# An attention kernel whose TensorE loop is written out, with values rounded in one GpSimd operation and the first keys and maxima on their own transfers

## The chip, the cores and the metric

One Trainium2 chip; the kernel runs on one of its cores. Five engines of that core have a part: TensorE (PE in the rows, its weight loads PEld), VectorE (DVE), ScalarE (ACT), GpSimd (POOL) and SyncE (SP), which issues the transfers. The metric is the device time of one execution in microseconds, lower is better.

## The reference

1600 queries (16 x 100 rows of 256) attend to 23104 keys made from a context, in 16 heads of 16, with queries, keys, probabilities and values rounded to 8-bit grids; a feed-forward layer with 8 experts follows.

```python
kv = (cond @ Wkv + bkv).reshape(1, -1, 2, H, hd)        # H = 16 heads, hd = 16
q = _fq_sym(q * scale, axis=-1)                         # round(q / s) * s, s = max|q| / 127
k = _fq_sym(k, axis=-1)
v = _fq_sym(v, axis=2)                                  # one step for each head and column of v
attn = softmax(q @ k.T)                                 # 1600 x 23104 for each head
attn = _fq_unsigned(attn, axis=-1)                      # step = row maximum / 255
x = x + (attn @ v) @ Wp + bp
x = x + ffn(layernorm(x))                               # 8 experts, two for each row
```

## The kernel before

Each engine has one program written by hand; semaphores tie them together. There are four stages.

**Preparation** (0 to 486 us): 51 steps of 512 rows project queries, keys and values. Three bf16 parts of the keys go to memory as `kT_parts`, float values as `v_float`, whole-number queries as `q_int` (`sp.dma_start(qi_d...)`, line 768).

**Prologue** (486 to 723 us). Two chains run beside each other. In one, TensorE multiplies the queries of the first block with all keys of head 0, a job at a time: `job` (line 1431) writes a pair of psum banks, VectorE's `job` (1292) reduces them to maxima in `mpart`. There are 96 + 7 such jobs, and two pairs of banks. The keys come in three pieces (`load_k1`). In the other chain the values are rounded in nine chunks of 2560 KB: load `vin` (three buffers, `load_vin`), GpSimd multiplies by `vinv` in place (line 1058), VectorE adds and takes away `RNE` to round, writing `vo` in f16 (`round_values`, line 1320, at chunks `ROUND_AT` of the other chain), SyncE stores `vo` (two buffers, `store_vo`). After the last chunk GpSimd rounds off with small constants, a memset over `K3` (line 1083) and two over `y` and `xh` (1090, 1091), which wait for the last stores. Then the maxima of block 0 are transposed (`mT`) and loaded as three rows of `QT` by SyncE (`load_m`, 841, `load_m_tail`, 847).

**Main loop** (723 to 8122 us): 16 heads x 4 blocks of 400 queries. A block is three bodies (`body(h, b, c)`), each with 15 groups of four key tiles of 128. For each tile TensorE makes scores (line 1522; the 181st tile of a block, `KX`, at 1548 opens the block) in a ring of three psum banks, ScalarE takes their exponential (1186; 1170 for `KX`), GpSimd rounds four of them at a time (1105). TensorE sums the group before with `ones` (1489) and multiplies the one before that with the values (1499). Between the tiles stand 78 jobs (1434) that find the maxima for a later block. All engines run the same nest through `bodies`: a hardware loop over `h` (line 402), in it one over `b` (404), and in that three bodies written out. Wait values are computed in registers. A tile with `j` in `PAIRS` waits for the exponential that frees the bank of its successor too, and the successor has no wait.

**Feed-forward layer** (8122 to 8735 us).

## Time and profile before

| | us |
|---|---|
| median of 3 runs | 8744.33 |
| lowest, highest | 8737.29, 8747.74 |
| the profiled execution | 8736.84 |
| its span | 8735.0 |
| preparation, prologue, main loop, feed-forward layer | 486, 237, 7399, 613 |
| TensorE busy | 93% of the span |
| VectorE, ScalarE, GpSimd busy | 77%, 62%, 60% |

A row of a group gives count, busy time, mean duration of one and the idle time ahead of it with the instruction that ended it. The chain of waits is read from the last instruction backwards: each piece is what held up the next. "issue" there is time in which an engine had nothing to wait for that the profile shows. Rows of PEldq, ACTq, DVEq and POOLq are instructions that the engine's sequencer handles alone (branches, register operations, waits).

### The profile page before, as it was taken

The page shows a single profiled execution, that of the slowest core. Times are in us where ns is not written, and L with a number is a line of the kernel's source. Part 1 is how long each engine was busy: PE and PEld are TensorE (multiplying, and loading weights), DVE is VectorE, ACT ScalarE, POOL GpSimd, SP SyncE. Part 2 cuts the span into 40 slices and gives each one's busy share as a digit, 9 for nine tenths or more (in the row PEclk, how much of TensorE's full clock was granted, in tenths as well). Part 3 has the DMA queues.
Part 4 walks back from the last instruction along what each step waited for, and adds up shares of the span by engine and source line. Part 5 has one row for each costly group of instructions (what it writes and reads, how often), then busy time and mean ns, then how long its engine had stood idle before and what let it go on. Part 6 is the DMA issues. An engine that isn't in the chain of part 4 may idle for free.

```text
span 8735.0 us, 208420 instructions
## 1 busy us (share of the span) xinstructions
PE 8114.0 (93%) x60567; PEld 2495.4 (29%) x60567; DVE 6754.0 (77%) x6609; ACT 5422.6 (62%) x12187; POOL 5211.0 (60%) x3573
## 2 busy tenths in 40 slices
PE   8937999999999999999999999999999999999688
PEld 4512222222222222222222222222222222222343
DVE  8977777777777777777777777777777777777666
ACT  2304667666666666666666666666666666666333
POOL 5765556555655566555555566555555566555356
PEclk9958999999999999999999999999999999999799
DMA  5663020202020201111110202020202021110000
GB/s 163 209 201 76 24 36 23 38 19 42 17 44 15 44 17 39 22 35 26 31 30 25 36 23 38 22 38 19 43 14 46 15 41 21 38 21 25 11 4 4
DMA packets 324119, 357.12 MB, mean 41 GB/s; under 512 B 66266, under 2 KB 306246, under 8 KB 315174
## 3 DMA queue, kind: packets, MB, share of 16 engines
q1 hardware_dynamic: 323046, 343.01, 17.0%
q8 instruction: 649, 10.63, 0.5%
q14 instruction: 424, 3.47, 0.1%
HBM read 264.31 MB, written 78.41 MB: 39 GB/s over the span
## 4 chain that ended last, share of the span: by engine, by line
PE 87%; issue 5%; DVE 4%; POOL 2%; DMA 1%; ACT 1%; SPq 0%; DVEq 0%; POOLq 0%; ACTq 0%
PE psum L1522 30%; PE psum L1489 27%; PE psum L1434 17%; PE psum L1499 6%; PE psum L1404 3%; POOL mix L431 1%; DVE mpart L1293 1%; DVE act_c L572 1%; PE psum L693 1%; PE psum L1481 1%; DVE vo L1320 1%; PE psum L1567 1%; PE psum L1416 0%; PE psum L666 0%; PE psum L1392 0%
## 5 line engine op out<-in xcount | busy, mean ns | idle before, releaser
L1293 DVE TENSOR_REDUCE mpart<-psum 128x1 f32<-128x978 f32 (+1 forms) x5095 | 5774.9, 1171 | 1581.6 <-PE psum L1434 1510.9
L1186 ACT ACTIVATE y<-psum 128x400 f32<-128x400 f32 x11520 | 5006.4, 506 | 2013.8 <-PE psum L1522 1922.2
L1105 POOL TENSOR_SCALAR xh<-y 128x1600 f16<-128x1600 f32 x2880 | 4397.8, 1527 | 2751.1 <-PE psum L1499 1698.0
L1522 PE MATMUL psum<-QT,K 99*128 x11520 | 3046.6, 346 | 39.1 <-ACT y L1186 37.8
L1489 PE MATMUL psum<-y,ones 128*17 128x400 f32 x23048 | 2573.5, 513 | 0.0
L1434 PE MATMUL psum<-K,QS 48*128 48x489 bf16 x8464 | 1510.4, 389 | 156.8 <-DVE mpart L1293 92.9
L1522 PEld LDWEIGHTS psum<-QT,K 99*128 99x128 bf16 x11520 | 796.8, 98 | 2381.6 <-ACT y L1186 1771.6
L1499 PE MATMUL psum<-xh,vwin 128*16 128x400 f16 x11528 | 1027.9, 338 | 0.5 <-POOL xh L1105 0.5
L1434 PEld LDWEIGHTS psum<-K,QS 48*128 48x128 bf16 x8464 | 372.5, 94 | 1202.1 <-issue 952.1
L1489 PEld LDWEIGHTS psum<-y,ones 128*17 128x17 f32 x23048 | 403.8, 96 | 794.3 <-issue 794.0
L1499 PEld LDWEIGHTS psum<-xh,vwin 128*16 128x16 f16 x11528 | 324.5, 91 | 637.6 <-POOL xh L1105 322.1
L572 DVE TENSOR_TENSOR act_c<-act_a,combB 128x400 f32<-128x400 f32 x256 | 314.3, 1300 | 53.1 <-ACT act_a L465 53.1
L1404 PE MATMUL psum<-wkv,srcT 128*128 128x512 f32 x736 | 324.7, 594 | 0.0
L431 POOL TENSOR_TENSOR mix<-mix,act_c 128x400 f32<-128x400 f32 x224 | 294.8, 1352 | 2.3 <-DVE act_c L572 2.3
L465 ACT ACTIVATE act_a<-psum,b1c 128x400 f32<-128x400 f32 x256 | 152.2, 594 | 166.5 <-PE psum L682 102.4
L1548 PE MATMUL psum<-QT,KX 99*128 x64 | 30.8, 481 | 235.4 <-issue 235.4
L682 PE MATMUL psum<-t1d,b1T 128*128 128x400 f32 x512 | 216.5, 531 | 18.6 <-ACT act_a L465 16.8
L1170 ACT ACTIVATE yx<-psum 128x400 f32<-128x400 f32 x64 | 32.3, 504 | 280.5 <-PE psum L1548 280.5
L427 POOL TENSOR_SCALAR mix<-act_c 128x400 f32<-128x400 f32 x32 | 24.1, 764 | 266.8 <-DVE act_c L572 266.8
L1404 PEld LDWEIGHTS psum<-wkv,srcT 128*128 128x128 f32 x736 | 136.8, 191 | 154.8 <-issue 154.8
L1028 POOL TENSOR_TENSOR kq<-kv,kinv 128x256 f32<-128x256 f32 x200 | 118.1, 623 | 89.2 <-DVE kinv L1242 89.2
L1434 PE MATMUL psum<-K,QL 48*128 48x489 bf16 x910 | 163.4, 379 | 3.3 <-DVE mpart L1293 2.8
(189 smaller groups left out, 2562.4 us busy)
## 6 DMA issues: line engine op xcount, KB each, us to landing
K<-kT_parts SPq DMA_DIRECT2D x288, 240.0 KB, 8.3
vwin<-v_int SPq DMA_DIRECT2D x579, 80.0 KB, 1.9
K1X<-kT_parts SPq DMA_DIRECT2D x772, 45.8 KB
kT_parts<-part SPq DMA_DIRECT2D x135, 256.0 KB, 3.0
src<-in_ctx_dram SPq DMA_DIRECT2D x46, 512.0 KB, 4.4
v_float<-kv SPq DMA_DIRECT2D x45, 512.0 KB, 5.0
vin<-v_float SPq DMA_DIRECT2D x9, 2560.0 KB, 14.6
K<-kT_parts SPq DMA_DIRECT2D x34, 450.9 KB
```

Of the source, the lines that this page charges most:

```text
L431: pool.tensor_tensor(mix[:, f, :], mix[:, f, :], act_c[:, i % CR, :], ALU.add).then_inc(mixed, 1)
L465: act.activation(act_a[:, i % AR, :], psum[:, bank, 0:QB], ACT.Gelu_apprx_tanh, bias=b1c[:, f:f + 1])\
L572: dve.tensor_tensor(act_c[:, i % CR, :], act_a[:, i % AR, :], combB[:, e, :], ALU.mult)\
L682: pe.matmul(psum[:, bank, 0:QB], b1T[:, f * P:(f + 1) * P], t1d[:, e, :], start=False, stop=True, skip_group_check=True).then_inc(p_ready, 1)
L1105: pool.tensor_scalar(xh[:, g % YR, :, :], y[:, g % YR, :, :], INT_STEP, 0.0, ALU.mult, ALU.add)\
L1186: act.activation(y[:, s % YR, j, :], s2_bank(GT * s + j), ACT.Exp).then_inc(exp_done, 1)
L1293: dve.tensor_reduce(mpart[:, t, column], buf[:, :, 0:CHALF], AX.XY, ALU.max).then_inc(s1_free, 1)
L1404: last = pe.matmul(kv_psum(t)[:, 0:width], srcT[:, k.r, c, t * P:(t + 1) * P], w, start=(c == 0), stop=(c == DC - 1))
L1434: last = pe.matmul(buf[:, k, 0:CHALF], tile[top:end, :], keys[top:end, :], start=True, stop=True)
L1489: last = pe.matmul(ACC[32 * j:32 * j + HD + 1, :], ones[:], y[:, g % YR, j, :], start=(start and j > 0), stop=True, skip_group_check=True)
L1499: last = pe.matmul(ACC[32 * j:32 * j + HD, :], vwin[:, g % GROUPS // 5, GT * (g % 5) + j, :], xh[:, g % YR, j, :], start=False, stop=True, ...
L1522: pe.matmul(s2_bank(t), K3[0:MROW, c * REGION + t * P:c * REGION + (t + 1) * P], queries, start=True, stop=True).then_inc(s2_ready, 1)
```

## The change

TensorE's nest becomes Python loops: 64 blocks x 3 bodies stand in the program, with no branch between them and constants as wait values; the other four engines keep their hardware loops. `PAIRS` goes: every tile waits for its own bank. In the prologue GpSimd multiplies by `vinv * 2^-24` and writes f16 `vo` straight, which rounds to whole steps of 2^-24, and VectorE's nine roundings go; `ones` carries the other factor. The keys of the first two chunks are loaded alone and before the queries, the store of `q_int` is split in two halves with a semaphore each, and the second half is moved behind the first value load and the rest of the first key piece. The first maxima are loaded by ScalarE's queue.

```diff
-PAIRS = (0,)
+K1_FIRST = CSTEP + CHALF
-ROUND_AT = (5, 7, 9, 11, 13, 15, 17, 19, 21)
...
             sp.wait_ge(qi_copied, DC)
-            for i in range(3):
-                for c in range(DC):
-                    sp.dma_start(qi_d[H // DC * c:H // DC * (c + 1), i, :, :], qintT[:, c, :]).then_inc(qi_stored, 16)
+            def store_qi(c):
+                for i in range(3):
+                    sp.dma_start(qi_d[H // DC * c:H // DC * (c + 1), i, :, :], qintT[:, c, :]).then_inc(qi_stored[c], 16)
+
+            store_qi(0)
             wait_prep_stores(sp)
-            sp.wait_ge(qi_stored, 48 * DC)
...
+            load_keys(0, 0, K1_FIRST, k1_first)
+            sp.wait_ge(qi_stored[0], 48)
             load_qs(QS, 0, 0, qs_in)
-            load_k1(0, 0)
             load_qs(QX, 0, BLOCKS * MAIN, qx_in)
             load_vin(0)
+            load_keys(0, K1_FIRST, K1_EDGES[1], k1_in[0])
+            store_qi(1)
+            load_vin(1)
             load_k1(0, 1)
-            load_vin(1)
+            sp.wait_ge(qi_stored[1], 48)
             load_vin(2)
             load_k1(0, 2)
...
-            sp.wait_ge(mt_copied, 1)
-            load_m(0, 0)
-            load_m_tail(0)
...
-                pool.memset(w[:, HD:HD + 1], INT_STEP).then_inc(zeroed, 1)
+                pool.memset(w[:, HD:HD + 1], INT_STEP * INT_STEP).then_inc(zeroed, 1)
...
-            pool.wait_ge(v_scaled, 2)
+            pool.wait_ge(v_scaled, 3)
             for c in range(9):
                 pool.wait_ge(vin_in[c % 3], 16 * (c // 3 + 1))
-                pool.tensor_tensor(vin[:, c % 3, :, :], vin[:, c % 3, :, :],
-                                   vinv[:].unsqueeze(1).to_broadcast([P, VCH, D]), ALU.mult).then_inc(vin_scaled, 1)
+                if c >= 2:
+                    pool.wait_ge(vo_stored[c % 2], 16 * (c // 2))
+                pool.tensor_tensor(vo[:, c % 2, :, :, :].rearrange("p h t d -> p t h d"),
+                                   vin[:, c % 3, :, :].rearrange("p t (h d) -> p t h d", h=H),
+                                   vinv[:].rearrange("p (h d) -> p h d", h=H).unsqueeze(1).to_broadcast([P, VCH, H, HD]),
+                                   ALU.mult).then_inc(vo_ready, 1)
...
             mt_copy(0, 0, 0, 4 * CHUNKS, s1_buf(4 * CHUNKS))
+            act.wait_ge(qs_split, 2)
+            load_m(act, 0, 0)
+            load_m_tail(act, 0)
...
+            dve.wait_ge(v_scaled, 2)
+            dve.tensor_scalar(vinv[:], vinv[:], INT_STEP, None, ALU.mult).then_inc(v_scaled, 1)
...
-                if chunk in ROUND_AT:
-                    round_values(ROUND_AT.index(chunk))
...
-                if piece_of(chunk) >= 0:
+                if chunk == 0:
+                    pe.wait_ge(k1_first, 32)
+                elif chunk == 2:
+                    pe.wait_ge(k1_in[0], 32)
+                elif piece_of(chunk) >= 0:
                     pe.wait_ge(k1_in[piece_of(chunk)], 32)
...
-                        if j in PAIRS:
-                            pe.wait_ge(exp_done, T + t + 2)
-                        elif j - 1 not in PAIRS:
-                            pe.wait_ge(exp_done, T + t + 1)
+                        pe.wait_ge(exp_done, T + t + 1)
...
-            bodies(pe, body, head_start)
+            for h in range(H):
+                head_start(h)
+                for b in range(BLOCKS):
+                    for c in range(BODY_C):
+                        body(h, b, c)
```

TensorE, from the last value group of a block to the first of the next. Before, the end of the loop's text (the branches go back to the second piece):

```order
L1499 MATMUL psum<-xh,vwin 16x400 x3
L404 REGISTER_ALU
L404 COMPARE_AND_BRANCH
L402 REGISTER_ALU
L402 COMPARE_AND_BRANCH
```

Before, the start of the loop's text:

```order
L404 UNCONDITIONAL_BRANCH [waits kx_in]
L1511 ISA [waits k_in0]
L1547 ISA [waits m_in]
L1548 ISA [waits exp_done]
L1548 ISA
L1548 MATMUL psum<-QT,KX 128x400
L1522 MATMUL psum<-QT,K 128x400 [waits exp_done]
L1522 MATMUL psum<-QT,K 128x400
```

Now, the same place between blocks 0 and 1:

```order
L1502 MATMUL psum<-xh,vwin 16x400 x3
L1548 MATMUL psum<-QT,KX 128x400 [waits exp_done,m_in,k_in0]
L1522 MATMUL psum<-QT,K 128x400 [waits exp_done] x2
L1433 MATMUL psum<-K,QL 128x489 [waits s1_free]
```

The branches and register operations are gone, and each of the two tiles has a wait of its own.

GpSimd in the prologue, chunks 1 to 3 of the values. Before:

```order
L1058 TENSOR_TENSOR vin<-vin,vinv 128x5120 [waits vin_in1]
L1058 TENSOR_TENSOR vin<-vin,vinv 128x5120 [waits vin_in2]
L1058 TENSOR_TENSOR vin<-vin,vinv 128x5120 [waits vin_in0]
```

Now:

```order
L1064 TENSOR_TENSOR vo<-vin,vinv 128x20x16x16 [waits vin_in1]
L1064 TENSOR_TENSOR vo<-vin,vinv 128x20x16x16 [waits vo_stored0,vin_in2]
L1064 TENSOR_TENSOR vo<-vin,vinv 128x20x16x16 [waits vo_stored1,vin_in0]
```

From chunk 2 on GpSimd itself now waits for the store that empties the `vo` buffer; VectorE did so before.

SyncE at the start of the prologue. Before:

```order
L768 DMA q_int<-qintT 8x16x1664 x5
L797 DMA QS<-q_int 48x384 [waits v_stored2,qi_stored,k_stored2,qs_split,v_stored1,k_turned,k_stored1,v_max,v_stored0,k_stored0]
L797 DMA QS<-q_int 48x384
L810 DMA K<-kT_parts 48x1x4810 x2
L797 DMA QX<-q_int 48x128 x2
L826 DMA vin<-v_float 128x5x1024
L810 DMA K<-kT_parts 48x1x4329 x2
L826 DMA vin<-v_float 128x5x1024 x2
```

Now:

```order
L821 DMA K<-kT_parts 48x1x970 [waits v_stored2,k_stored2,qs_split,v_stored1,k_turned,k_stored1,v_max,v_stored0,k_stored0]
L821 DMA K<-kT_parts 48x1x970
L809 DMA QS<-q_int 48x384 [waits qi_stored0]
L809 DMA QS<-q_int 48x384
L809 DMA QX<-q_int 48x128 x2
L840 DMA vin<-v_float 128x5x1024
L821 DMA K<-kT_parts 48x1x3840 x2
L779 DMA q_int<-qintT 8x16x1664 x3
L840 DMA vin<-v_float 128x5x1024
```

The first keys and queries stand ahead of half of the `q_int` store, and the second value load stands behind the other half.

## Rows read from the trace of the kernel before

**Rows 1.** The page: busy time, the chain by engine, TensorE's instruction transfers.

```profile
PE 8114.0 (93%) x60567; PEld 2495.4 (29%) x60567; DVE 6754.0 (77%) x6609; ACT 5422.6 (62%) x12187; POOL 5211.0 (60%) x3573
...
PE 87%; issue 5%; DVE 4%; POOL 2%; DMA 1%; ACT 1%; SPq 0%; DVEq 0%; POOLq 0%; ACTq 0%
...
q8 instruction: 649, 10.63, 0.5%
```

**Rows 2.** Waits of 720 to 8120 us: total, times, longest.

```profile
PE psum L1548 <- issue: 235.4, 64, 18.9
```

**Rows 3.** Line 404, 4060 to 4080 us: ns (min/median/max), first and last start.

```profile
L404 PEldq COMPARE_BRANCH  x1: 3457/3457/3457, 4069.4 to 4069.4; - x1
...
L404 ACTq COMPARE_BRANCH  x1: 45/45/45, 4069.6 to 4069.6; - x1
...
L404 DVEq COMPARE_BRANCH  x1: 56/56/56, 4069.9 to 4069.9; - x1
L404 DVEq FUSED_REGOPS  x1: 160/160/160, 4070.2 to 4070.2; - x1
...
L404 ACTq FUSED_REGOPS  x1: 133/133/133, 4072.1 to 4072.1; - x1
```

**Rows 4.** Chain of waits, 4070 to 4100 us: start, length, what.

```profile
4070.73 3.06 issue
...
4074.96 0.93 PE psum L1434 x4
4075.89 0.78 PE psum L1522 x2
4076.68 1.47 PE psum L1489 x8
...
4078.48 0.78 PE psum L1522 x2
...
4090.02 0.56 PE psum L1434 x4
4090.58 0.45 PE psum L1522 x2
4091.02 0.80 PE psum L1489 x8
```

**Rows 5.** Stretches: length, busy time by engine, granted clock, DMA share, GB/s.

```profile
4074.00:4076.00 2.00, 2.00 (x8) 0.42 (x7) 0.47 (x1) 1.30 (x3) 0.53 (x1) 0.50 0.00 0
...
4080.00:4082.00 2.00, 1.98 (x14) 0.58 (x12) 2.00 (x3) 1.85 (x5) 0.69 (x1) 1.00 0.03 8
```

**Rows 6.** Timeline, 4060 to 4080 us: start, length, engine, instruction, idle before.

```profile
4074.33 0.50 ACT L1170 ACTIVATE yx<-psum 128x400 f32<-128x400 f32 x1 [4.10 <-PE psum L1548]
```

**Rows 7.** Groups, 486 to 723 us: busy, mean ns, idle before.

```profile
L1293 DVE TENSOR_REDUCE mpart<-psum 128x1 f32<-128x978 f32 x103 | 112.5, 1161 | 34.4 <-PE psum L1434 34.4
...
L1320 DVE TENSOR_SCALAR vo<-vin 128x5120 f16<-128x5120 f32 x9 | 56.2, 6246 | 2.2 <-POOL vin L1058 2.2
```

**Rows 8.** Line 1058: ns of one, min/median/max.

```profile
L1058 POOL TENSOR_TENSOR vin<-vin,vinv x9: 10952/13017/13555, 536.2 to 659.3; 128x5120 f32<-128x5120 f32 x9
```

**Rows 9.** Chain of waits of the whole span, in the prologue.

```profile
525.46 32.10 DMA vin<-v_float
...
681.56 2.73 DVE vo L1320
...
721.49 1.52 issue
```

**Rows 10.** Timeline of GpSimd, 530 to 725 us.

```profile
693.23 0.30 POOL L1063 MEMSET vox<- 64x256 f16 x1 [19.75 <-DVE vox L1332]
```

**Rows 11.** Stretches of the prologue.

```profile
600.00:640.00 40.00, 13.55 (x46) 2.38 (x46) 40.00 (x25) 0.00 (x0) 34.70 (x4) 0.50 0.90 300
```

**Rows 12.** The page: transfers, with KB of one and median us to landing.

```profile
vin<-v_float SPq DMA_DIRECT2D x9, 2560.0 KB, 14.6
...
v_int<-vo SPq DMA_DIRECT2D x9, 1280.0 KB, 13.9
```

More of the change, by code:

```diff
@@ L315, in build @@
         v_absmax, v_scaled = sem("v_absmax"), sem("v_scaled")
-        vin_scaled, vo_ready = sem("vin_scaled"), sem("vo_ready")
+        vo_ready = sem("vo_ready")
         vin_in, vo_stored = [sem(f"vin_in{j}") for j in range(3)], [sem(f"vo_stored{j}") for j in range(2)]
-        vx_in, vx_scaled, vx_round, vx_zero, vx_stored = sem("vx_in"), sem("vx_scaled"), sem("vx_round"), sem("vx_zero"), sem("vx_stored")
-        qi_kept, qs_kept, qi_turned, qi_copied, qi_stored = (
-            sem("qi_kept"), sem("qs_kept"), sem("qi_turned"), sem("qi_copied"), sem("qi_stored"))
+        vx_in, vx_round, vx_zero, vx_stored = sem("vx_in"), sem("vx_round"), sem("vx_zero"), sem("vx_stored")
+        qi_kept, qs_kept, qi_turned, qi_copied = sem("qi_kept"), sem("qs_kept"), sem("qi_turned"), sem("qi_copied")
+        qi_stored = [sem(f"qi_stored{c}") for c in range(DC)]
+        k1_first = sem("k1_first")
         k1_in, k1x_in = [sem(f"k1_in{r}") for r in range(3)], [sem(f"k1x_in{j}") for j in range(2)]
@@ L373, in key_window, with load_m, load_m_tail @@
             return keys[:, CSTEP * chunk:CSTEP * chunk + CHALF]
+        def load_m(eng, ring, b):
+            for r in range(3):
+                eng.dma_start(QT[NROW + r:NROW + r + 1, ring, ds(b * QB, MAIN)].rearrange("r (t c) -> r t c", c=P),
+                             mT[(PT + 1) * r:(PT + 1) * r + PT, :]).then_inc(m_in, 16)
+        def load_m_tail(eng, ring):
+            for r in range(3):
+                row = (PT + 1) * r + PT
+                eng.dma_start(QT[NROW + r:NROW + r + 1, ring, :].rearrange("r (b k) -> r b k", b=BLOCKS)[:, :, MAIN:QB],
+                             mT[row:row + 1, 0:BLOCKS * TAIL].rearrange("r (b k) -> r b k", b=BLOCKS)).then_inc(mx_in, 16)
         def s2_bank(j):
@@ L805, in load_tiles, with load_keys, load_k1 @@
                     load_qs(dst, (h + (turn + ahead) // BLOCKS) % H, (turn + ahead) % BLOCKS * MAIN, arrived)
-            def load_k1(head, piece):
-                first, end = K1_EDGES[piece], K1_EDGES[piece + 1]
+            def load_keys(head, first, end, arrived):
                 for k, (top, bottom) in enumerate(HALVES):
                     sp.dma_start(K1[top:bottom, first:end], kT_d[:, ds(head * HD, HD), HALF * k + first:HALF * k + end])\
-                        .then_inc(k1_in[piece], 16)
+                        .then_inc(arrived, 16)
+            def load_k1(head, piece):
+                load_keys(head, K1_EDGES[piece], K1_EDGES[piece + 1], k1_in[piece])
             def load_k1x(head, chunk, j):
@@ L837, in load_values @@
                              v_d[ds(body, 1), :, :].rearrange("a p n -> (a p) n")).then_inc(v_in[q], 16)
-            def load_m(ring, b):
-                for r in range(3):
-                    sp.dma_start(QT[NROW + r:NROW + r + 1, ring, ds(b * QB, MAIN)].rearrange("r (t c) -> r t c", c=P),
-                                 mT[(PT + 1) * r:(PT + 1) * r + PT, :]).then_inc(m_in, 16)
-            def load_m_tail(ring):
-                for r in range(3):
-                    row = (PT + 1) * r + PT
-                    sp.dma_start(QT[NROW + r:NROW + r + 1, ring, :].rearrange("r (b k) -> r b k", b=BLOCKS)[:, :, MAIN:QB],
-                                 mT[row:row + 1, 0:BLOCKS * TAIL].rearrange("r (b k) -> r b k", b=BLOCKS)).then_inc(mx_in, 16)
+            load_keys(0, 0, K1_FIRST, k1_first)
+            sp.wait_ge(qi_stored[0], 48)
             load_qs(QS, 0, 0, qs_in)
-            load_k1(0, 0)
             load_qs(QX, 0, BLOCKS * MAIN, qx_in)
             load_vin(0)
+            load_keys(0, K1_FIRST, K1_EDGES[1], k1_in[0])
+            store_qi(1)
+            load_vin(1)
             load_k1(0, 1)
-            load_vin(1)
+            sp.wait_ge(qi_stored[1], 48)
             load_vin(2)
@@ L938, in block @@
                             sp.sem_inc(sp_passed, 1)
-                            load_m((h + (1 if end else 0)) % 3, 0 if end else b + 1)
+                            load_m(sp, (h + (1 if end else 0)) % 3, 0 if end else b + 1)
                             if end:
-                                load_m_tail((h + 1) % 3)
+                                load_m_tail(sp, (h + 1) % 3)
                         if q == 2 and c == BODY_C - 1:
```

12 lines of the change are left out of this document (1 added, 11 removed).

## The prediction

> **What bounds the kernel now.** I read the page first: TensorE is busy for 93% of the span and makes 87% of the chain, with "issue" at 5% next [rows 1]. So TensorE's own work is the bound, and the 5% are time in which it waited for no data. The list of waits says where most of that is: the tile that opens a block (line 1548) finds TensorE idle for 235.4 us in 64 blocks [rows 2]. Without the first (18.9 us, the end of the prologue) that is 216.5 us over 63 block edges, 3.44 us each.
>
> The rows of line 404 at one edge say why [rows 3]. TensorE's branch back takes 3457 ns; VectorE's takes 56 ns and the next instruction stands there 0.3 us after it. ScalarE's branch takes 45 ns too, but its next instruction comes at 4072.1, 2.6 us after the branch at 4069.6. The long loops (TensorE, ScalarE) get their code anew at the branch, the short one doesn't. ScalarE's wait is covered today, because TensorE is away longer: it starts `KX` at 4073.79 [rows 4], and ScalarE is then idle on TensorE, not the other way round [rows 6].
>
> The second cost of an edge is the clock. It is granted at 0.50 behind the gap (the lower level, 1.2 GHz) and is back at 1.00 by 4080 [rows 5]. In the chain the same operations take 0.93, 0.78 and 1.47 us behind the gap and 0.56, 0.45 and 0.80 us later in the block [rows 4], a ratio of 1.81/3.18 = 0.57. The slow stretch runs from 4073.79 to 4078.48 + 0.78 = 4079.26, 5.47 us, and would take 3.1 us at full clock: 2.4 us lost. An edge costs 3.44 + 2.4 = 5.8 us.
>
> The prologue ends at 721.49 + 1.52 = 723.0 [rows 9]. Its chain goes through value load 1 (there at 525.46 + 32.10 = 557.6), then VectorE, which alternates 103 jobs (112.5 us) with nine roundings (56.2 us) [rows 7] and ends the last rounding at 681.56 + 2.73 = 684.3. GpSimd sits idle for 19.75 us on VectorE before its constants [rows 10], and from there to the first block it is 723.0 - 693.2 = 29.8 us of GpSimd's own work.
>
> **The loop written out.** The branch goes, 64 times: 63 gaps of 3.44 us, and the overlap of two matmuls that an idle engine lacks, 0.07 us (a pair of tiles takes 0.45 us where it follows other work). What is late next is ScalarE. It keeps its loop, and I expect its code at the same place after the branch. At this edge TensorE ends at 4070.73. It can do `KX`, two tiles and two jobs without ScalarE, 0.17 + 0.45 + 0.56 - 0.1 for the overlap, until about 4071.8; the next tile needs the bank that `KX` holds. ScalarE is ready at 4072.1 + 0.13 for the register operation and 0.1 for its wait, 4072.4, and needs 0.50 us for `KX` [rows 3, 6], so the bank is free at 4072.9. TensorE idles 1.1 us, and about 0.25 us more for the tile behind it, since ScalarE hands out banks one by one. That is 1.35 us here; for edges where the code comes later I take 1.5 on the mean (bounds 1.0 and 2.2: code half a microsecond sooner, or as late as the branch that TensorE itself pays, shorter by the lead that ScalarE has). VectorE, free at 4070.2, covers its two banks, and GpSimd isn't asked for before the next group.
>
> Does the clock still fall? The gap is cut from 3.06 us to 1.1, with work close before and behind it. Behind gaps of 3.06 it fell. The gaps inside a block (0.3 us and less) never let it fall. 1.1 us lies between, nearer to the second; I take no fall. The Trainium skill ("TensorE: Matmul & The Clock Gate", section "Why this matters for your kernels") asks for no idle gaps over about 3 us between bursts, or the clock goes to half; the trace agrees for 3.06 us, and no row shows 1.1 us.
>
> So an edge gives 3.44 + 2.4 + 0.07 - 1.5 = 4.4 us, and 63 of them 278 us (bounds 3.7 and 4.9: 233 and 309).
>
> The size of a loop that runs without new code can be read in the Trainium skill too ("Runtime: NRT & Kernel Launch", "Instruction fetch mechanics"): two blocks of 256 instructions for all engines but TensorE. ScalarE's loop has fewer than 512 instructions, and by that rule it would not fetch, the 1.5 us would fall away, and the kernel would take about 95 us less than my sum. The rows show a ScalarE that fetches, so the measurement decides.
>
> The constants cost and save nothing: register operations run on TensorE's sequencer, which reached the branch at 4069.4 while its array worked until 4070.73, so it is 1.3 us ahead. Waits of their own for the tiles of a pair: 0. The first tile of a pair waited for a bank that was free long before, and pairs with a wait on each take 0.45 us as those with one. Loads of keys, queries and maxima are in place before an edge today, and edges that come 3 us sooner relative to them leave that so for all but the second part of the maxima, which has about 1 us to spare at a head's start.
>
> **The prologue.** (a) VectorE loses 56.2 us of roundings and gets one multiplication of some 0.3 us before the prologue. Its chain is then 103 jobs of 1.09 us, 112 us. The first eight start early, the others wait for the rest of the first key piece; even if that came at 535 us, 95 jobs end at 640, before GpSimd's chain, so this side is free. (b) GpSimd takes one operation per chunk as before. Alone it takes 10.95 us, beside VectorE's rounding 13.55 [rows 8]; now it is alone. That its output is f16 in another order is not in the trace; I take 11 us (bounds 11 and 13.5). (c) The transfers: a chunk is 2560 KB in and 1280 KB out [rows 12], 3.84 MB. At the best rate of the prologue, 300 GB/s with a DMA share of 0.90 [rows 11], that is 12.8 us, more than GpSimd's 11. GpSimd's new wait for the store two chunks back asks for 13.9 + 11 us per two chunks [rows 12, 8], 12.5 each, with nothing queued behind it but its own next chunk, so it takes the same place. Chunks 1 to 5 go at 12.8 us, the last three, with no load beside them, at 11, and the key region that is loaded between takes 1.44 MB / 300 = 5 us: 64 + 33 + 5 = 102. (d) The start: queries and keys are issued about 8 us sooner, but value load 1 has gone behind the rest of the keys and half of `q_int`. It lands between 545 (all gained) and 557.6 (as now); I take 551. Last chunk at 551 + 102 = 653, 31 us sooner than 684.3. Behind it GpSimd has the small remainder (1 us) and its 29.8 us: first block at 684, instead of 723. The maxima on ScalarE's queue free SyncE for some 5 us that no one waits for. Gain 39 us; bounds 59 (545, all chunks at 11) and 21 (557.6, all at 13.5).
>
> **Sum.** 8735.0 - 278 - 39 = 8418 us of span, 8420 for an execution that is profiled (1.8 around the span). The median of before is 7.5 us above its profiled execution; half of that added gives 8424. With both bounds of the terms: 8370 to 8485.
>
> **Rivals.** (1) *The clock falls all the same.* ScalarE's gap of 1.1 to 1.6 us, near the smaller gaps around it, is enough. Then 63 x 2.4 = 151 us come back: 8575. For it: the slow stretch is long against the gap, so little may set it off. (2) *Another wait takes the whole place of the branch*, so an edge stays as it is and the prologue alone gains: 8705. It needs an engine that is ready only 3 us after TensorE's end; ScalarE at 1.4 us speaks against it. (3) *ScalarE's code comes sooner* once TensorE fetches none beside it, up to the rule above: 8329. (4) *Slower: the straight code stalls.* TensorE gets its code in 649 transfers of 16.4 KB [rows 1]; about 530 of them fall in the main loop, 8 a block. They were asked for inside a body before too, and no row there shows a stall. If each now held TensorE up, the limit is 317/530 = 0.6 us apiece; at the 3.4 us of a branch [rows 3] it would be 1800 us and 10200 in all. It would have to be something that a program written out has and a body written out hasn't.
>
> **How the numbers follow.** My forecast has 0.74, rival 1 has 0.12, rival 2 has 0.05, rival 3 has 0.05, rival 4 has 0.04. The range has to reach rival 1 to leave out no more than 2 in 10: 8370 to 8580, with 0.14 outside. A measurement of this kernel can tell 0.2% (17 us) from no change. Faster: 0.95; within 0.2%: 0.01; slower: 0.04.
>
> **What would show it.** In the changed kernel: no branch of TensorE in the main loop; `KX` without idle time before it; the third tile of a block waiting for ScalarE 1 to 1.6 us; ScalarE's first instruction of a block as late as now against its branch; granted clock 1.00 from the second group of the first block to the end of the loop. 111 us from block to block instead of 115.6. In the prologue: operations of 11 us on GpSimd, VectorE done by 640, the first block at 684. If the clock row shows a dip at each edge, rival 1 holds; if `KX` waits for "issue", rival 4; if value chunks run at 13 us or more, the f16 output or the store's wait was priced too low.

## The result and the profile of the changed kernel

The changed kernel takes 8446.6 us (median of 4 runs, 8446.4 to 8454.8) where the kernel before takes 8746.0 beside it (8737.3 to 8753.1): a ratio of 0.966, 95% interval 0.964 to 0.968, 299 us less. Forecast were 8424, with a range from 8370 to 8580. The profiled execution has a span of 8444.7 us, 290.3 less than the 8735.0 of before.

| Part, from the profiled executions | before | after | difference |
|---|---|---|---|
| first `KX` starts | 723.0 | 708.2 | -14.8 |
| 63 periods, from first to last `KX` | 7282.9 (115.60 each) | 7003.6 (111.17 each) | -279.3 |
| from the last `KX` to the end | 729.1 | 732.8 | +3.7 |

So the loop gave what was forecast (278) and the prologue 15 us of 39.

The page, against [rows 1]: TensorE works for less time and a larger share, ScalarE's part of the chain has gone from 1% to 2%, and TensorE's instruction transfers have fallen from 649 to 462.

```profile
span 8444.7 us, 192076 instructions
...
PE 7981.2 (95%) x60567; PEld 2495.3 (30%) x60567; DVE 6720.7 (80%) x6600; ACT 5409.1 (64%) x12187; POOL 5195.9 (62%) x3573
...
q8 instruction: 462, 7.57, 0.4%
...
PE 87%; issue 4%; DVE 2%; POOL 2%; ACT 2%; DMA 1%; SPq 1%; ACTq 0%; DVEq 0%; POOLq 0%
```

Waits from 690 to 8120 us (total, times, longest), the place of [rows 2]. The 235.4 us behind the branch are gone. Of the 85.2 us for line 1548, 53.4 are the one wait at the prologue's end; the rest is half a microsecond of weight load per block beside other work. New is the wait for `yx`: 69.1 us in 64 blocks, 1.08 each.

```profile
PEld psum L1548 <- issue: 85.2, 64, 53.4
...
PE psum L1522 <- ACT yx L1181: 69.1, 64, 1.6
```

One edge in the rows of the loop's line (now 415; ns, then first and last start), 4040 to 4050 us. TensorE has no row there. ScalarE's branch takes 45 ns and the register operation behind it stands 2.4 us later, as in [rows 3].

```profile
L415 ACTq COMPARE_BRANCH  x1: 45/45/45, 4043.7 to 4043.7; - x1
...
L415 ACTq FUSED_REGOPS  x1: 133/133/133, 4046.1 to 4046.1; - x1
```

The chain at that edge (start, length, what) goes through just that time, 1.73 us in which ScalarE waited for nothing that is shown, and on to `yx`:

```profile
4044.40 1.73 issue
4046.12 0.13 ACTq L415
...
4046.38 0.05 ACT yx L1181
```

Stretches of the edge (columns as in [rows 5]). TensorE works for 1.03 of the two microseconds from 4046 and its clock stays at 1.00; in [rows 5] it was at 0.50 behind the gap.

```profile
4044.00:4046.00 2.00, 2.00 (x19) 0.49 (x11) 1.60 (x3) 0.40 (x2) 1.34 (x1) 1.00 0.15 28
4046.00:4048.00 2.00, 1.03 (x12) 0.37 (x14) 2.00 (x2) 1.62 (x5) 0.72 (x2) 1.00 0.05 17
```

In the prologue, GpSimd's timeline (start, length, engine, what, idle before and its releaser): chunk 1 is in at 542.3, but chunk 2 waits 28 us, for a store.

```profile
542.34 10.97 POOL L1064 TENSOR_TENSOR vo<-vin,vinv 128x5120 f16<-128x5120 f32 x1 [19.02 <-DMA vin<-v_float]
581.56 10.96 POOL L1064 TENSOR_TENSOR vo<-vin,vinv 128x5120 f16<-128x5120 f32 x1 [28.25 <-DMA v_int<-vo]
...
625.16 21.88 POOL L1064 TENSOR_TENSOR vo<-vin,vinv 128x5120 f16<-128x5120 f32 x2 [7.47 <-DMA v_int<-vo]
657.30 21.88 POOL L1064 TENSOR_TENSOR vo<-vin,vinv 128x5120 f16<-128x5120 f32 x2 [10.27 <-DMA v_int<-vo]
```

SyncE's queue shows why. Chunk 0 was ready in `vo` at 523.3. SyncE then still had keys, queries and two more value loads to issue, and came to its store at 562.6; the data were out at 581.4.

```profile
534.98 12.14 SPq L821 DMA_DIRECT2D K<-kT_parts  x2
547.16 4.12 SPq L809 DMA_DIRECT2D QL<-q_int  x2
551.32 0.73 SPq L866 DMA_DIRECT2D vinx<-v_float_last  x1
552.10 9.99 SPq L830 DMA_DIRECT2D K1X<-kT_parts  x4
562.13 0.46 SPq L840 DMA_DIRECT2D vin<-v_float  x1
562.64 3.96 SPq L846 DMA_DIRECT2D v_int<-vo  x1
```

### The profile page after: what moved, and what is told of

The parts are those of the page before. It is cut to its first block, busy times and chain, and to the rows that moved or that the text cites. A ratio compares the mean times of both kernels' runs of the same rounds, so it can differ in the third digit from the quotient of the medians.

```text
span 8444.7 us, 192076 instructions
## 1 busy us (share of the span) xinstructions
PE 7981.2 (95%) x60567; PEld 2495.3 (30%) x60567; DVE 6720.7 (80%) x6600; ACT 5409.1 (64%) x12187; POOL 5195.9 (62%) x3573
## 4 chain that ended last, share of the span: by engine, by line
PE 87%; issue 4%; DVE 2%; POOL 2%; ACT 2%; DMA 1%; SPq 1%; ACTq 0%; DVEq 0%; POOLq 0%
PE psum L1522 30%; PE psum L1492 26%; PE psum L1433 17%; PE psum L1502 6%; PE psum L1403 3%; ACT y L1197 2%; POOL mix L442 1%; DVE act_c L583 1%; PE psum L704 1%; DMA v_int<-vo 1%; PE psum L1484 1%; PE psum L1567 1%; PE psum L1415 1%; PE psum L677 1%; PE psum L1391 0%
## 5 line engine op out<-in xcount | busy, mean ns | idle before, releaser
L1522 PE MATMUL psum<-QT,K 99*128 99x400 bf16 x11520 | 2991.8, 339 | 111.4 <-ACT yx L1181 69.1
L1492 PE MATMUL psum<-y,ones 128*17 128x400 f32 x23048 | 2528.5, 506 | 0.0
L1433 PE MATMUL psum<-K,QS 48*128 48x489 bf16 x8464 | 1481.9, 380 | 88.6 <-DVE mpart L1306 34.4
L1522 PEld LDWEIGHTS psum<-QT,K 99*128 99x128 bf16 x11520 | 798.7, 97 | 2413.4 <-ACT y L1197 1700.2
L1144 ACT ACTIVATE part<-rest 128x1024 bf16<-128x1024 f32 x50 | 52.9, 1058 | 168.0 <-DVE rest L1264 168.0
L1064 POOL TENSOR_TENSOR vo<-vin,vinv 128x5120 f16<-128x5120 f32 x9 | 98.6, 10963 | 84.4 <-DMA v_int<-vo 49.2
```

Source lines behind the costliest of these rows:

```text
L1433: last = pe.matmul(buf[:, k, 0:CHALF], tile[top:end, :], keys[top:end, :], start=True, stop=True)
L1492: last = pe.matmul(ACC[32 * j:32 * j + HD + 1, :], ones[:], y[:, g % YR, j, :], start=(start and j > 0), stop=True, skip_group_check=True)
L1522: pe.matmul(s2_bank(t), K3[0:MROW, c * REGION + t * P:c * REGION + (t + 1) * P], queries, start=True, stop=True).then_inc(s2_ready, 1)
```

## Experiments

Times are medians; the ratio is against the kernel before on the same chip, with its 95% interval. "Period" is the mean time from one `KX` to the next in the profiled execution, "first" the start of the first.

| Run | Time, us | Ratio | Span | First | Period |
|---|---|---|---|---|---|
| changed kernel | 8446.6 | 0.966 (0.964 to 0.968) | 8444.7 | 708.2 | 111.17 |
| e1_loop_alone | 8464.6 | 0.969 (0.967 to 0.970) | 8466.9 | 722.8 | 111.29 |
| e2_prologue_alone | 8761.7 | 1.003 (1.002 to 1.004) | 8767.4 | 706.6 | 116.33 |
| e6_prologue_pairs | 8734.2 | 0.999 (0.998 to 1.000) | 8730.1 | 707.8 | 115.65 |
| e4_gap_after_kx | 8674.9 | 0.994 (0.992 to 0.995) | 8663.1 | 706.7 | 114.62 |
| e8_gap_tile3 | 8561.1 | 0.980 (0.979 to 0.982) | 8544.9 | 707.8 | 112.75 |
| e3_act_out | 8450.6 | 0.967 (0.966 to 0.969) | 8450.2 | 707.8 | 111.27 |
| e5_act_out_sem | 8337.7 | 0.954 (0.953 to 0.956) | 8340.1 | 708.3 | 109.57 |
| e7_stores_on_act | 8445.7 | 0.967 (0.965 to 0.968) | 8446.6 | 700.7 | 111.37 |
| e9_constants_early | 8337.8 | 0.954 (0.953 to 0.956) | 8336.1 | 689.0 | 109.77 |
| e10_act_stores_consts | 8334.6 | 0.954 (0.953 to 0.955) | 8330.8 | 685.3 | 109.77 |
| e11_loads_behind | 8331.9 | 0.954 (0.952 to 0.955) | 8330.7 | 683.0 | 109.78 |
| e12_ffn_loads_late | 8317.5 | 0.951 (0.950 to 0.953) | 8318.9 | 684.0 | 109.59 |

### The two halves of the change apart

The loop alone, on the kernel before:

```diff
-            bodies(pe, body, head_start)
+            for h in range(H):
+                head_start(h)
+                for b in range(BLOCKS):
+                    for c in range(BODY_C):
+                        body(h, b, c)
```

> The kernel before with one edit: TensorE's loop nest written out (its pair waits, the prologue and all else stay). Theory (the two parts of the change add up, and the loop gives 4.4 us at each of 63 edges): 279 us less than before, 8735 - 279 = 8456 for the profiled span, 111.2 us from block to block, first block at 723. Rival (the first keys, the values and the constant waits of the tiles have a share in the gain of the loop): less than 270 us.

The period falls by 4.31 us, 272 us in 63, with the pair waits and the old prologue in place. That is the gain of the loop but for 8 us, of which 6 are in the clock (27 us at the lower clock at three edges, against 14 us at four). So the waits of their own for the two tiles of a pair are worth at most the 0.12 us per block that remain between the two, as forecast: nothing that can be told. The span is 268 us under that of before, 11 short of the theory's 279 and just inside the rival's "less than 270"; but only these 8 us are in the loop, and the clock explains 6 of them, so the reason that the rival gives is not shown.

The other half alone, the changed kernel with TensorE on its hardware loop:

```diff
-            for h in range(H):
-                head_start(h)
...
+            bodies(pe, body, head_start)
```

> The changed kernel with TensorE back on the hardware loop. Theory: the prologue's part alone, 723.0 - 708.2 = 15 us less than before (8720 of span), edges as before: 3.4 us idle, then the lower clock, 115.6 us from block to block. By the prediction's own term it would have been 39 us (8696). Rival (the time won in the prologue is lost again behind it, since later transfers meet others): no difference from before.

Neither held. The first block starts 16.4 us sooner, and the kernel is slower than before, by 0.3%. The period has grown to 116.33. The rows of TensorE's branch, 730 to 8000 us, of the kernel before and then of this one (ns, minimum/median/maximum):

```profile
L404 PEldq COMPARE_BRANCH  x62: 83/3614/4137, 833.5 to 7886.1; - x62
```

```profile
L415 PEldq COMPARE_BRANCH  x62: 82/4608/5157, 817.7 to 7914.1; - x62
```

A branch of 4.6 us instead of 3.6. What differs on TensorE in the loop is only that each tile of a pair has its wait, with a register operation each: 2873 instructions more in the trace than before, 45 a block. To see that it is this, I gave that kernel its pair waits back:

```diff
-                        pe.wait_ge(exp_done, T + t + 1)
+                        if j in PAIRS:
+                            pe.wait_ge(exp_done, T + t + 2)
+                        elif j - 1 not in PAIRS:
+                            pe.wait_ge(exp_done, T + t + 1)
```

> The kernel before with the prologue of the changed one, hardware loops and pair waits kept. It differs from e2_prologue_alone by the waits of the tiles alone. Theory (the wait per tile makes TensorE's loop 45 instructions a block longer, and its branch 4.6 us instead of 3.6): idle time at an edge back at 3.4 us, 115.6 us from block to block, first block at 707, 8718, 16 us less than before and 44 less than e2_prologue_alone. Rival (the prologue or its placement of loads slows the edges): 8762 as e2_prologue_alone.

```profile
L416 PEldq COMPARE_BRANCH  x63: 82/3637/4132, 818.4 to 7988.9; - x63
```

The theory held: 3.6 us again, the idle time at an edge back from 4.42 to 3.48, the period from 116.33 to 115.65, 27 us off the median. TensorE's instruction transfers fit it: 649 before, 702 in e2_prologue_alone, 649 again here. So the same waits are free in code written out and cost some 0.7 us a block in the loop, through what the branch back then takes. That it is the length of the code which sets this, and not where its pieces come to lie, is argued: one length was tried. Against the kernel before, the prologue is worth 0.1%, 8 us, with an interval that ends at nothing: the first block starts 15 us sooner, but from the last `KX` to the end it took 736.6 us here, for 729.1 before. This stretch took between 729.0 and 736.6 us in the profiles of this document, so a few microseconds of it can't be put down to an edit.

### How long may TensorE stand still

Rival 1 was that the clock falls at the shorter gaps too. Two versions of the changed kernel widen the gap with no branch in it, by a wait for GpSimd's operation on `yx`. The first, behind `KX`:

```diff
                         pe.matmul(s2_bank(S2_RING - 1), KX[0:MROW, h % 2, :], queries, start=True, stop=True)\
                             .then_inc(s2_ready, 1)
+                        pe.wait_ge(rounded_yx, B + 1)
```

> The changed kernel with one more wait: behind KX TensorE waits until GpSimd has scaled yx (rounded_yx), with no branch on TensorE. At the edge near 4045 us KX ends at 4045.1 and GpSimd's operation at 4047.6, so TensorE idles some 2.6 us there instead of 1, and the third tile comes 1.7 us later. Theory A (the length of the gap alone makes the clock fall): 63 x (1.7 + 2.4) = 258 us over the changed kernel, about 8705, with a lower clock at each edge. Theory B (the fall needs the branch, or a gap of 3 us and more): 63 x 1.7 = 107 us, about 8555, clock at 1.00.

The second, two tiles and two jobs later:

```diff
+                    if s == 0 and c == 0:
+                        pe.wait_ge(rounded_yx, B + 1)
                     score_tile(s, 2)
```

> The changed kernel with the wait for rounded_yx ahead of the third tile instead of behind KX. At the edge near 4045 us TensorE would be idle from 4046.0 to 4047.75, 1.7 us instead of 0.9, and tile three is 0.8 us later. e4_gap_after_kx showed that 2.6 us with no branch makes the clock fall. Theory A (the fall needs more than 2 us): 63 x 0.8 = 50 us, 8497, clock at 1.00. Theory B (any gap over the 1.1 us of the changed kernel does it): 63 x (0.8 + 2) = 175 us, 8620.

Stretches around one edge of each (columns as in [rows 5]), first with the wait behind `KX`, then ahead of the third tile:

```profile
4144.00:4146.00 2.00, 2.00 (x19) 0.62 (x17) 1.88 (x3) 1.40 (x4) 1.32 (x2) 1.00 0.01 4
4146.00:4148.00 2.00, 0.17 (x1) 0.00 (x0) 0.46 (x1) 0.32 (x1) 1.19 (x1) 1.00 0.18 37
4148.00:4150.00 2.00, 1.02 (x4) 0.26 (x6) 0.00 (x0) 0.66 (x3) 0.52 (x1) 0.50 0.02 4
```

```profile
4090.00:4092.00 2.00, 1.48 (x15) 0.38 (x7) 1.59 (x2) 0.01 (x1) 1.52 (x1) 1.00 0.17 41
4092.00:4094.00 2.00, 0.71 (x2) 0.13 (x2) 1.58 (x2) 1.45 (x4) 0.52 (x1) 0.83 0.01 4
4094.00:4096.00 2.00, 2.00 (x14) 0.44 (x14) 0.00 (x0) 0.73 (x2) 0.99 (x1) 0.50 0.00 0
4096.00:4098.00 2.00, 2.00 (x12) 0.41 (x10) 0.92 (x1) 1.55 (x4) 0.54 (x1) 0.82 0.00 0
```

Over the 63 edges of each kernel, counted from the clock and matmul records of its one profiled execution. For e8_gap_tile3 and e4_gap_after_kx these were the fastest executions, and the others had a lower mean clock (0.961 to 0.964 against 0.965, and 0.954 to 0.956 against 0.957), so the usual time at the lower clock is somewhat longer there than in the table:

| Kernel | idle at an edge, mean us | edges where the clock fell | time at the lower clock, us |
|---|---|---|---|
| e5_act_out_sem (below) | none | 0 | 0 |
| changed kernel | 1.09 | 4 | 14 |
| e8_gap_tile3 | 1.80 | 46 | 178 |
| e4_gap_after_kx | 2.65 | 52 | 324 |
| before | 3.44 | 63 | 413 |

It needs no branch: a gap alone lets the clock fall, as theory A of e4_gap_after_kx had it (8675 measured, 8705 expected, 8555 by the other). It isn't one threshold either: e8_gap_tile3, at 8561, lies between its theories (8497 and 8620), since at 1.80 us most edges fall, but for a short time. Over the kernels, longer gaps fall more often and for longer. (The gap isn't at the same place in all: ahead of `KX` before, behind it in e4_gap_after_kx, ahead of the third tile in the changed kernel and in e8_gap_tile3.) In e4_gap_after_kx the period grew by 3.45 us: 1.56 of idle time, and 310 us more at the lower clock, 4.9 an edge, which at the ratio 0.57 of the slow stretch cost 0.43 x 4.9 = 2.1. The two make 3.7. In e8_gap_tile3 it is 0.71 + 0.43 x 2.6 = 1.8 against 1.58 measured.

Inside one kernel the length of a gap tells less. The four falls of the changed kernel are at its four longest gaps, 1.40 to 1.57 us, and the next longest is 1.28. But in e1_loop_alone the clock fell at gaps of 1.19 and 1.23 us and not at one of 1.58, and the 17 edges of e8_gap_tile3 that kept the clock had gaps of 1.62 to 2.22 us, as long as the others. So the changed kernel, with a mean of 1.09 us, was already at the foot of the slope. That was a narrower escape than the chance of 0.12 says. The Trainium skill ("TensorE: Matmul & The Clock Gate", section "Why this matters for your kernels") asks for no idle gaps over about 3 us; here gaps of 1.6 to 2.2 us between dense work already let it fall at 46 of 63 edges, so for this kernel the rule is too generous.

### What is left at an edge

ScalarE's loop written out as well, so that no long loop branches:

```diff
-            bodies(act, body)
+            for h in range(H):
+                for b in range(BLOCKS):
+                    for c in range(BODY_C):
+                        body(h, b, c)
```

> The changed kernel with ScalarE's loop nest written out as well. Theory (the code that ScalarE gets behind its branch is all that is left of an edge): the wait for yx at the third tile goes, 1.1 us of it and some 0.2 to 0.4 us of the waits behind it, 63 x 1.3 = 82 us less than the changed kernel, about 8365 (8350 to 8378). Rival A (straight code of ScalarE stalls it, some two transfers a block of 2.6 us each): no gain or slower than 8447. Rival B (VectorE or GpSimd at their own branches are late next): half the gain, about 8405.

The wait at the edge is gone, the clock never falls, and the time is that of the changed kernel. None of the three expectations covers it: nothing stalls long, no other engine is late at the edge. The time has gone into the whole block. In the waits from 690 to 8120 us, of the changed kernel and then of this one, weight loads wait 1468 times more for an exponential and 248 us longer:

```profile
PEld psum L1522 <- ACT y L1197: 1700.2, 3844, 1.0
```

```profile
PEld psum L1525 <- ACT y L1197: 1948.6, 5312, 0.9
```

One pair of tiles in each timeline shows the size. In the changed kernel the exponential starts 0.38 us after its tile, here 0.46:

```profile
4061.50 0.51 PE L1522 MATMUL psum<-QT,K 99*128 99x400 bf16 x2
...
4061.88 1.69 ACT L1197 ACTIVATE y<-psum 128x400 f32<-128x400 f32 x4 [0.51 <-PE psum L1522]
```

```profile
4062.57 0.51 PE L1525 MATMUL psum<-QT,K 99*128 99x400 bf16 x2
...
4063.03 1.69 ACT L1197 ACTIVATE y<-psum 128x400 f32<-128x400 f32 x4 [0.59 <-PE psum L1525]
```

From 1000 to 7600 us some 2,550 exponentials in each of the two kernels open a group and found ScalarE idle; their median is 380 ns in the changed kernel and 461 ns here. The instruction records name the cause. A group's first exponential waits for three things: its tile, and two results that are old (`summed`, `rounded_y`). With register values the two old waits stand on instructions ahead, and the tile's wait is on the exponential. With constants, the three are put on the exponential and one semaphore instruction ahead of it, and it is the tile's wait that lands on the separate instruction: it passes when the tile is there, and only then comes the exponential. An increment behind the two old waits gives them an instruction of their own:

```diff
                     act.wait_ge(summed, groups_before(h, b, c) + s + 1)
                     act.wait_ge(rounded_y, groups_before(h, b, c) + s + 1)
+                    act.sem_inc(act_passed, 1)
```

> The version with ScalarE's loop written out (e3_act_out), plus one semaphore increment behind the two waits for old results (summed, rounded_y) at the head of each group of four exponentials, so that these two get an instruction of their own and the wait for the tile (s2_ready) stays on the exponential. In e3_act_out the wait for the tile stood on a separate instruction ahead, and the first exponential of a group began 461 ns after its tile's start instead of 380. Theory (that 81 ns, at most 46 times a block, ate what the edge gave): back at 380 ns, the gain of the edge comes through, 63 x 1.1 = 70 us less than e3_act_out, 8380. Rival (the written-out code of ScalarE costs time in another way): 8450 as e3_act_out.

The start is back at 380 ns and the time at 8337.7, 113 us under e3_act_out and 109 under the changed kernel. That is more than the 70 expected. The period is 1.60 us shorter than in the changed kernel: the 1.08 in which TensorE stood still, and half a microsecond more. I put that down to a ScalarE that was behind at each edge and had to catch up. It fits that weight loads wait 36 us less for exponentials (1664.1 us for 1700.2), but no run takes this part by itself.

### The prologue

The stores of the rounded values go to ScalarE's queue, which is empty there:

```diff
-                sp.wait_ge(vo_ready, c + 1)
-                sp.dma_start(v_d.rearrange("(h c) p n -> c p h n", c=9)[c, :, :, :],
+                act.wait_ge(vo_ready, c + 1)
+                act.dma_start(v_d.rearrange("(h c) p n -> c p h n", c=9)[c, :, :, :],
```

> The changed kernel with the nine stores of the rounded values issued by ScalarE instead of SyncE. Theory (the first store waits in SyncE's queue: value chunk 0 is ready at 523.3, its store is issued at 562.6, and GpSimd's chunk 2 waits for it until 581.6 though its load is there at 559.9): chunk 2 starts at 560, the rest follow at 12.8 us or so, first block at 686 to 690, 18 to 22 us less than the changed kernel, 8426. Rival (the transfers themselves are the limit, 0.93 share and 275 GB/s from 600 to 640 us): the earlier store only delays the key and value loads beside it, first block at 700 or later, under 8 us.

GpSimd's timeline of this kernel:

```profile
561.05 10.98 POOL L1058 TENSOR_TENSOR vo<-vin,vinv 128x5120 f16<-128x5120 f32 x1 [7.73 <-DMA vin<-v_float]
580.72 10.97 POOL L1058 TENSOR_TENSOR vo<-vin,vinv 128x5120 f16<-128x5120 f32 x1 [8.69 <-DMA vin<-v_float]
597.48 21.89 POOL L1058 TENSOR_TENSOR vo<-vin,vinv 128x5120 f16<-128x5120 f32 x2 [5.80 <-DMA v_int<-vo]
638.94 21.88 POOL L1058 TENSOR_TENSOR vo<-vin,vinv 128x5120 f16<-128x5120 f32 x2 [19.57 <-DMA v_int<-vo]
```

Chunk 2 starts at 561.05 instead of 581.56, as the theory said: of its wait of 28 us, 20.5 were SyncE's queue, and the rest is the wait for its own load. Then 13 of these 20.5 us are lost again: chunk 6 (the last row; chunks 4 and 5 share the row above, while the expectation of e11_loads_behind below calls it chunk 5 and counts the 47 us of its store from the end of chunk 3) waits 19.6 us for the store of chunk 4, ready at 608.4 and out at 638.8, 30 us later. The transfers are full there (a share of 1.01 from 620 to 640 us). The first block starts 7.5 us sooner, at 700.7, which is what the rival had (700 or later, under 8 us), and the median is the same as without. In the profile the 7.5 us went in the loop, which is 13 us longer, with 41 us at the lower clock instead of 14 (12 us); why the clock fell at six edges and not at four stays open (five of the six have gaps of 1.39 to 1.59 us, one has 1.17).

GpSimd's small constants, 23.5 us of its tail, now stand ahead of chunk 2 (on e5_act_out_sem):

```diff
             for c in range(9):
+                if c == 2:
+                    constants()
+                    pool.wait_ge(ones_ready, 2)
                 pool.wait_ge(vin_in[c % 3], 16 * (c // 3 + 1))
```

> The version with ScalarE's loop written out and the semaphore increment (e5_act_out_sem, 8337.7), with GpSimd's 23.5 us of small constants and the memset over K3 moved ahead of value chunk 2, where GpSimd stood idle for 28 us in the changed kernel. Theory (those 23.5 us were on the path that ends the prologue and are covered there): first block at 708.3 - 23.5 = 685, 8314. Rival (the queries, keys or values of the first block land later than GpSimd now ends, up to 699 us in the changed kernel): first block at 700, 8330.

The first block starts at 689.0, 19 us sooner, and the kernel takes as long as without: 8337.8 and 8337.7. The rival was right that the loads are late next, but it isn't the first block's start that waits. The waits of 688 to 810 us have a transfer among them, for the values of the second body:

```profile
PE psum L1510 <- DMA vwin<-v_int: 14.6, 1, 14.6
```

SyncE issues these values at 748.0, behind 40 us of loads for the feed-forward stage and the queries of a later head; its queue again:

```profile
698.88 4.05 SPq L900 DMA_DIRECT2D bp_r<-in_L_xattn_bp_dram  x1
...
729.85 7.94 SPq L916 DMA_DIRECT2D b2n<-in_L_ffn_B_dram  x16
...
748.02 0.38 SPq L850 DMA_DIRECT2D vwin<-v_int  x1
```

The first block took 128.1 us for 115.4. The next two runs put both prologue edits together, and then load the first queries, `KX` and the first key region behind the value loads:

> e5_act_out_sem with the value stores on ScalarE's queue as in e7_stores_on_act, and GpSimd's constants ahead of value chunks 0 and 1. Theory (the two gains add: 7.5 us by the stores, 23.5 us by the constants): first block at 708.3 - 31 = 677, 8307. Rival as in e9_constants_early (the loads of the first block are late next): first block at 690 or later, 8320 or more.

> e10_act_stores_consts with the first queries, the key tile KX and the first key region loaded behind the value loads, not between them. Theory (after 560 us the transfers are the limit: chunk 5 of the values waited 19.6 us in e7_stores_on_act for a store that took 47 us beside these loads): that wait falls under 10 us, the last chunk ends some 10 us sooner, first block at 667 to 672, 8299. Rival (the values' own 3.84 MB a chunk fill the transfers, the moved loads only come later): first block where e10_act_stores_consts has it.

They start at 685.3 and 683.0, not at the 677 and 667 to 672 of the theories, and both give their gain back in the same way (12.5 and 12.9 us of waiting for `vwin`): 8334.6 and 8331.9, within 6 us of the version without them. Moving the loads was worth 2.3 us, not 10: GpSimd waits 2.8 us ahead of chunk 6, but 12.6 ahead of chunk 7. So from 560 us on, GpSimd waits for value transfers, whatever the order of the others. Their rate alone doesn't explain it: in e11_loads_behind the DMA share is 1.10 from 620 to 640 us, but 0.60 and 0.56 in the 20 us on either side. How much of it is the turn of load, operation and store through two `vo` buffers is not taken apart; a third buffer was not tried.

Last, the loads of the feed-forward weights go between the blocks of the last head:

```diff
-            for third in range(3):
-                load_ffn(third)
...
+            load_ffn(0)
             with sp.Fori(0, 2) as b:
                 block(H - 1, b, True)
             for b in range(2, BLOCKS):
+                load_ffn(b - 1)
                 block(H - 1, b, True, b)
```

> e11_loads_behind with the loads of the feed-forward weights (29 of them, SyncE issues them from 698 to 738 us) moved into the last head, a third ahead of each of three places between its blocks. Theory (a prologue that ends sooner gave nothing, since SyncE reaches the values of the second body only at 748 us behind these loads, and the first block took 128 us in e9_constants_early instead of 110; the value group waited 14.6 us): first block at 683 as in e11_loads_behind and 110 us long, 17 us less, 8315. Rival (the weight loads now hold SyncE up between the last blocks as long, where TensorE waits just so): no change, 8332, with the lost time at the end of the loop.

The theory held, but for 3 us: 8317.5, 14.4 us less, the wait for `vwin` is gone and the first block takes 115.3 us. The 6 us over the others are its start at the lower clock, which the prologue leaves behind. This is the best version: 0.951 of the kernel before (0.950 to 0.953), 129 us under the changed kernel.

## Why the prediction was right, and where not

**An edge of before, 5.8 us.** Right. e4_gap_after_kx shows the two parts apart, idle time and clock, and its period follows from them. The ratio 0.57 priced the clock to within 0.3 us of a period.

**What is late next.** Right: ScalarE, by 1.08 us (forecast 1.1 from one edge and its rows), and with what is behind it 1.60, shown by e5_act_out_sem; I had taken 1.5. The period is 111.17 (forecast 111). This step could be worked out since the profile of before showed ScalarE's next instruction 2.6 us after its branch, though nobody waited for it then.

**No fall of the clock.** Right with four exceptions in 63, but in part by luck, and for a weaker reason than given. "1.1 us lies between, nearer to the second" compares 3.06 with 0.3; the longest gap inside a block of before is in fact 0.6 us (`PE psum L1522 <- ACT y L1186: 37.8, 64, 0.6` in its waits). And nearness decides nothing: e8_gap_tile3, with 0.7 us more of idle time, brings back some 70 us by the clock. The prediction gave the wait bounds of 1.0 to 2.2 us and priced the clock apart from it, as a rival; a wait in the upper half of these bounds would likely have brought a good part of the rival with it.

**Constants and pair waits at nothing.** Right for the change as made. e1_loop_alone bounds the pair waits at 0.12 us a block; the constants come with the loop written out, and that they cost nothing on TensorE is not shown by itself. Neither is a general truth: in the hardware loop the pair waits cost 0.7 us a block (e2_prologue_alone), and on ScalarE the constants moved a wait and cost 1.7 (e3_act_out against e5_act_out_sem). No rule of the prediction asked how long the code of a loop is.

**ScalarE's code.** The rule of two blocks of 256 instructions (the Trainium skill, "Runtime: NRT & Kernel Launch", "Instruction fetch mechanics") would, as I read it, have had no fetch in a loop of less than 512 instructions. The trace after still shows 2.4 us from branch to next instruction, and e5_act_out_sem shows that 101 us of the loop hung on it. The measurement decides, as it did in the prediction. The reading may be at fault and not the rule: ScalarE's block has 463 instructions, and a stretch of that length can lie across three blocks of 256. No run here moves it.

**The loads.** As forecast, none is waited for in the main loop of the changed kernel. It was nearer than thought at the start: a first block 19 us sooner runs into the values of the second body. The kernel's own 15 us did not.

**The prologue, 15 of 39 us, outside the bounds of 21 to 59.** By its steps: (a) VectorE's side was free, as said, though its last job ended at 656.8 and not by 640 (below). (b) 10.96 us for each operation with its f16 output in another order: 11 was right. (d) Value load 1 was there at 542.3, better than the 551 taken. The step that failed is (c), "asks for 13.9 + 11 us per two chunks [rows 12, 8], 12.5 each, with nothing queued behind it but its own next chunk". It counts a store from its issue, as if it were issued when the chunk is ready. I looked at what is queued behind GpSimd's wait, and not at what is queued ahead of the store on SyncE: the first store came 39 us late (562.6; in e7_stores_on_act 522.7). From chunk 1's load to the last chunk's end it took 679.2 - 542.3 = 137 us instead of 102. Of these 35 us, e7_stores_on_act, where the queue is gone, gives back 7.5 (the last chunk ends at 671.7); the larger rest goes with the second error of (c), the best rate of the prologue, 300 GB/s, taken for all of it. From 542 to 679 us the changed kernel moved 30.8 MB at 225 GB/s on the mean; at 300 they would have taken 103 us, about the 102 forecast, so it is the rate that was taken too high. The DMA share was 0.74, so the engines were not full throughout, and what kept the rate down is not taken apart. The tail of GpSimd was 29 us, as priced. The bound of 59 us leaves out the 5 us of the key region that the sum has; with them it is 54.

**The sum.** With its true sizes, 8735.0 - 279.3 - 14.8 + 3.7 = 8444.6, the span measured but for 0.1. It is 27 us over the 8418 forecast: 24 of the prologue and 4 behind the loop, less 1 of the loop. The median misses by 22, since it lies 2 us above that span and not 6.

**Rivals.** (1) The clock: at four edges here, and at 46 with 1.80 us of idle time. (2) Another wait takes the place of the branch: no. (3) ScalarE's code sooner: not by itself, the median from its branch to its next instruction is 2.5 us for 2.6 before (and 3.1 in e2_prologue_alone, where TensorE's branch takes longest); written out and with its waits in order it gives 109 us, where the rival had 95. (4) Straight code stalls TensorE: no sign of it. `KX` never waited behind the first, and there are 187 instruction transfers fewer than before, three for each of the 63 edges: before, the branch had to fetch code again.

## To carry to other kernels

Ahead of writing a loop out, look in the profile at each engine's first instruction behind its own branch, covered or not: the next one late is found there, and how long TensorE then stands still decides about the clock too: at a mean of 1.09 us it fell at 4 of 63 edges here, at 1.80 at 46. In code with constant waits, keep the wait that ends last on the instruction itself, and give the old ones an instruction of their own. And price a wait for a store or a load by what stands ahead of it in the queue that issues it: twice here a gain was held back by SyncE, which had 39 and 40 us of other transfers to issue first.

## What the runs showed of the hardware

- TensorE's branch back got dearer with a longer loop: 45 instructions a block more took its median from 3.6 to 4.6 us, and back when they went.
- An exponential whose last wait stands on the instruction ahead of it starts 81 ns later (461 for 380 ns), and some 43 such starts a block cost 1.7 us a block, as much as all that ScalarE's branch cost at an edge (1.6).
- The clock's fall is graded over these kernels: mean idle times of 1.09, 1.80, 2.65 and 3.44 us gave 14, 178, 324 and 413 us at the lower clock in 63 edges.
- VectorE's own small operations were held up by GpSimd in the prologue of the changed kernel. Two of 128x4 elements, 0.46 and 0.96 us long before, took 11 us each, and each ended with an operation of GpSimd (625.16 to 647.04 for the two):

```profile
625.17 10.97 DVE L1317 TENSOR_SCALAR mx<-mx 128x4 f32<-128x4 f32 x1
636.17 10.88 DVE L1320 CAST m<-mx 128x4 bf16<-128x4 f32 x1
```

  The reductions that read psum ran beside GpSimd at their usual 1.17 us. The Trainium skill ("SBUF — State Buffer", section "SBUF: two separate sides") has VectorE, in its modes that use two ports, and GpSimd share a pair of ports that one of them holds for a whole instruction while the other is blocked; the trace agrees for these two. Without their 20 us VectorE would have been done at 636, not at 656.8, so by the 640 of the prediction. It is also the likely reason that GpSimd's operations took 13 us instead of 11 beside VectorE's roundings before [rows 8].
